# Attention with a layer norm in front: scores in two groups of three units over three PSUM banks instead of three groups of two, with other steps moved in each engine's order

## The reference

```python
h = jnp.maximum(_layernorm(x, axis=-1), 0.0)
q = _heads(h @ Wq + bq)
k = _heads(h @ Wk + bk)
v = _heads(h @ Wv + bv)
scores = jnp.einsum('bhqd,bhkd->bhqk', q, k) / np.sqrt(HEAD_SIZE)
bias = jnp.where(graph_mask, 0.0, NEG)[:, None]
probs = jax.nn.softmax(scores + bias, axis=-1)
ctx = jnp.einsum('bhqk,bhkd->bhqd', probs, v)
out = x + ctx @ Wf + bf
```

## Time and profile before

| | us |
|---|---|
| three executions: median (lowest to highest) | 593.15 (592.7 to 593.23) |
| the profiled execution | 594.17 |
| its span, first to last instruction | 592.4 |
| PE busy in it | 575.3 |
| ACT, POOL, DVE busy | 516.3, 491.4, 473.5 |

### The profile page before, as it was taken

The page is one execution under the profiler, slowest core; times in us unless marked ns, Lnnn a source line. Parts: engine busy times, 40 slices in busy tenths (PEclk is TensorE's granted clock), DMA queues, the critical chain, the costliest instruction groups (busy, mean ns, idle before and its releaser), DMA issues.

```text
span 592.4 us, 17738 instructions
## 1 busy us (share of the span) xinstructions
PE 575.3 (97%) x6640; PEld 429.6 (73%) x6640; DVE 473.5 (80%) x1484; ACT 516.3 (87%) x1161; POOL 491.4 (83%) x533
## 2 busy tenths in 40 slices
PE   7997999999999999999999999999999999999986
PEld 7676777777777777777777777776777777777754
DVE  5988888888878878888887888888787778878664
ACT  2788999899999999999999999998999999999972
POOL 2779998888899888889988888988888898888870
PEclk9999999999999999999999999999999999999999
DMA  8048889879788989879897977789897787978662
GB/s 273 8 77 148 134 169 177 170 159 168 165 148 157 185 157 178 167 141 168 160 184 157 181 163 150 159 158 177 165 178 166 157 151 161 179 132 153 125 133 73
DMA packets 275640, 92.01 MB, mean 155 GB/s; under 512 B 257633, under 2 KB 275554, under 8 KB 275554
## 3 DMA queue, kind: packets, MB, share of 16 engines
q1 hardware_dynamic: 274352, 90.87, 79.8%
q10 hardware_dynamic: 1202, 0.01, 0.1%
HBM read 17.05 MB, written 12.58 MB: 50 GB/s over the span
## 4 chain that ended last, share of the span: by engine, by line
PE 82%; DVE 6%; ACT 5%; DMA 3%; issue 2%; POOL 1%; ACTq 0%; SPq 0%; DVEq 0%; POOLq 0%
PE ring L1043 18%; PE ring L1045 18%; PE ring L1044 18%; PE scores L1106 11%; PE ctx L1129 5%; PE ring L1141 3%; PE ctx L1131 3%; PE ctx L1130 3%; DMA p_cols<-p_rows 2%; DVE logits L750 2%; ACT probs L550 2%; DVE h_rows L767 1%; DMA bf_row<-in_L_gnn_bf_dram 1%; ACT qk L575 1%; PE ring L1171 1%
## 5 line engine op out<-in xcount | busy, mean ns | idle before, releaser
L428 POOL TENSOR_TENSOR p_rows<-probs,p_rows 128x512 f16<-128x512 f32 x190 | 220.6, 1161 | 32.2 <-ACT p_rows L555 31.8
L750 DVE CUSTOM_DVE_ANT_0 logits<-scores,mask,logit_unscale 128x256 f32<-128x256 f32 x384 | 169.0, 478 | 61.6 <-PE scores L1106 61.4
L550 ACT ACTIVATE probs<-logits,raised 128x256 f32<-128x256 f32 x372 | 168.9, 501 | 6.0
L1043 PE MATMUL ring<-h_cols,w_hi 128*128 128x256 f16 x576 | 157.2, 273 | 0.0
L1045 PE MATMUL ring<-h_cols,w_lo 128*128 128x256 f16 x576 | 157.0, 273 | 0.0
L1044 PE MATMUL ring<-h_cols,w_hi 128*128 128x256 f16 x576 | 156.9, 272 | 0.0
L414 POOL TENSOR_TENSOR split<-qk,split 128x512 f16<-128x512 f32 x96 | 111.5, 1161 | 36.4 <-DVE split L774 36.4
L555 ACT ACTIVATE p_rows<-probs 128x512 f16<-128x512 f32 x190 | 119.7, 630 | 6.0
L575 ACT ACTIVATE qk<-ring,qk_bias_s,qkv_ratio 128x256 f32<-128x256 f32 x192 | 96.5, 552 | 3.7 <-PE ring L1045 3.7
L1129 PEld LDWEIGHTS ctx<-v_hi,p_cols 128*128 128x128 f16 x756 | 68.9, 97 | 33.2 <-issue 27.7
L1129 PE MATMUL ctx<-v_hi,p_cols 128*128 128x65 f16 x756 | 88.2, 195 | 4.1 <-DMA p_cols<-p_rows 2.0
(11 more groups left out here) (116 smaller groups left out, 1158.6 us busy)
## 6 DMA issues: line engine op xcount, KB each, us to landing
x_in<-in_x_dram SPq DMA_DIRECT2D x32, 384.0 KB, 3.9
out_dram<-result SPq DMA_DIRECT2D x62, 192.0 KB, 2.2
p_cols<-p_rows SPq DMA_TRANSPOSE x190, 3.2
adj_in<-in_adj_dram SPq DMA_DIRECT2D x32, 64.0 KB, 2.9
w_raw<-in_L_gnn_Wq_dram SPq DMA_DIRECT2D x1, 576.0 KB, 5.6
w_raw<-in_L_gnn_Wv_dram SPq DMA_DIRECT2D x1, 576.0 KB, 8.0
w_raw<-in_L_gnn_Wf_dram SPq DMA_DIRECT2D x1, 576.0 KB, 9.0
h_cols<-h_rows SPq DMA_TRANSPOSE x29, 4.7
```

Source lines behind the costliest of these rows:

```text
L428: pool.tensor_tensor(p_rows[u][:, 1], probs[u % 3][:], p_rows[u][:, 0], ALU.subtract).then_inc(p_lo_ready, 1)
L550: act.activation(probs[u % 3][:, a], logits[u % 3][:, a], ACT.Exp, bias=raised[u % 3][:, a:a + 1], scale=-1.0).then_inc(probs_ready, 1)
L750: dve.tensor_tensor_reduce(out=logits[u % 3][:, a], in0=score_bank[a][:, u % 2 * S:(u % 2 + 1) * S], in1=mask[b.parity][:, t], scale=logit ...
L1043: pe.matmul(out_ap, a_hi, m_hi, start=first, stop=False)
```

## The change

- The scores banks are three, `scores0` to `scores2`; the third is the bank that was `peaks`. A group of scores is the three units of one query tile, 18 matmuls, at `attend(0)` and `attend(3)`. Unit 0 writes banks 1 and 2, unit 1 banks 0 and 2, unit 2 banks 0 and 1. Bank 1 is thus written by the lower half of the array for unit 0 and by the upper half for unit 2, so unit 2's first matmul of head 1 waits for a new semaphore, `shared_bank_done`, which the last matmul of unit 0 and head 0 raises.
- Batch 0 makes its scores in four groups, of the units 0 and 1, 2, 3, and 4 and 5.
- DVE: `mask_and_max` of unit 2 stands ahead of `v_lo_part`, `h_lo_rows` behind unit 3 and `divide` instead of behind unit 2, `layer_stats` ahead of `qk_hi_part`. ACT: `h_hi_rows` stands behind unit 2 instead of ahead of `context_hi` and unit 2. POOL: `add_bias` (the next input) stands behind `probs_lo` of unit 4, and `split_lo` of pair 2 ahead of it. SP: the transpose of unit 2 stands ahead of that of `h`.
- The last batches use other banks, and on DVE the division of batch 30 stands ahead of `mask_and_max` of unit 1 of batch 31.

```diff
-    GROUPS = UNITS // 2
+    GROUPS = UNITS // C
-        score_bank = [bank("scores0"), bank("scores1")]
-        peak_bank = bank("peaks")
+        score_bank = [bank(f"scores{n}") for n in range(3)]
+        peak_bank = score_bank[2]
...
+        def score_of(u, a):
+            n, column = ((1, 0), (2, 0), (0, 0), (2, S), (0, S), (1, S))[u % C * 2 + a]
+            return score_bank[n][:, column:column + S]
...
+        def scored(b, u):
+            if b.k == 0:
+                return (1, 1, 2, 3, 4, 4)[u]
+            return 4 + (b.k - 1) * GROUPS + u // C + 1
@@ SP, cycle @@
+                if here:
+                    transpose_probs(b, 2)
                 if (b + 2).exists():
                     transpose_h(b + 2)
-                if here:
-                    transpose_probs(b, 2)
@@ POOL, cycle @@
                 if here:
                     probs_lo(b, 3)
                 if front:
+                    split_lo(b + 1, 2)
+
+                if here:
+                    probs_lo(b, 4)
+                if front:
                     add_bias(b + 1)
-
-                if here:
-                    probs_lo(b, 4)
-                if front:
-                    split_lo(b + 1, 2)
@@ ACT, cycle @@
                 if front:
                     qk_full(b + 1, 0)
+                if before:
+                    context_hi(b + -1, 0)
+                if here:
+                    exps(b, 2)
+                    probs_hi(b, 2)
                 if (b + 2).exists():
                     h_hi_rows(b + 2)
-                if before:
-                    context_hi(b + -1, 0)
-                if here:
-                    exps(b, 2)
-                    probs_hi(b, 2)
@@ DVE, cycle @@
                 if here:
+                    mask_and_max(b, 2)
                     v_lo_part(b, 0)
                     v_lo_part(b, 1)
                 if b.k == 1:
                     weights_lo(3, 8)
-                if here:
-                    mask_and_max(b, 2)
+                if (b + 3).exists():
+                    layer_stats(b + 3, (0,))
                 if front:
                     qk_hi_part(b + 1, 0)
                 if before:
                     context_lo(b + -1, 0)
-                if (b + 2).exists():
-                    h_lo_rows(b + 2)
                 if here:
                     mask_and_max(b, 3)
                 if before:
                     divide(b + -1, 1)
+                if (b + 2).exists():
+                    h_lo_rows(b + 2)
                 if front:
                     qk_hi_part(b + 1, 1)
-                if (b + 3).exists():
-                    layer_stats(b + 3, (0,))
-
                 if here:
                     mask_and_max(b, 4)
-                if front:
-                    qk_hi_part(b + 1, 2)
                 if (b + 3).exists():
                     layer_stats(b + 3, (1,))
                     layer_moments(b + 3)
+                if front:
+                    qk_hi_part(b + 1, 2)
@@ DVE, last batch @@
             mask_and_max(LAST, 0)
+            divide(PREV, 0)
             mask_and_max(LAST, 1)
-            divide(PREV, 0)
+            mask_and_max(LAST, 2)
             finish(PREV + -1, 1)
             v_lo_part(LAST, 0)
             v_lo_part(LAST, 1)
-            mask_and_max(LAST, 2)
@@ PE @@
+            def scores(b, units):
+
+                for u in units:
...
+                wait(pe, logits_ready, b.count(2 * UNITS, 2 * units[0]))
+                for u in units:
                     t, tile = u // C, split[b.parity][u % C]
                     for n, (q, k) in enumerate(((1, 2), (1, 3), (0, 2))):
                         for a in range(2):
+                            if u % C == 2 and n == 0 and a == 1:
+
+                                wait(pe, shared_bank_done, b.count(GROUPS, u // C + 1))
                             own = slice(D * a, D * a + D)
+                            mm = pe.matmul(score_of(u, a), tile[own, q, t * P:(t + 1) * P], tile[own, k],
                                            start=(n == 0), stop=(n == 2))
+                            if u % C == 0 and n == 2 and a == 0:
+                                mm.then_inc(shared_bank_done, 1)
                 mm.then_inc(scores_ready, 1)
@@ PE, batch 0 @@
-            scores(Batch(0), 0)
+            pe.wait_ge(peaks_joined, 2)
+            scores(Batch(0), (0, 1))
...
-            scores(Batch(0), 1)
+            scores(Batch(0), (2,))
...
+            scores(Batch(0), (3,))
             project_qk(Batch(1), 1)
-            scores(Batch(0), 2)
+            scores(Batch(0), (4, 5))
@@ PE, cycle @@
-                    if here and u % 2 == 0:
-                        scores(b, u // 2)
+                    if here and u % C == 0:
+                        scores(b, range(u, u + C))
@@ PE, last batch @@
-            scores(LAST, 0)
+            scores(LAST, range(0, C))
             apply_probs(PREV, 2)
             project_out(PREV + -1, 1)
             apply_probs(PREV, 3)
-            scores(LAST, 1)
             transpose_context(PREV, 0)
             apply_probs(PREV, 4)
-            scores(LAST, 2)
+            scores(LAST, range(C, UNITS))
             apply_probs(PREV, 5)
```

More of the change, by code:

```diff
@@ L201, in gnn_attention @@
         scores_ready = sem("scores_ready")
+        shared_bank_done = sem("shared_bank_done")
         logits_ready = sem("logits_ready")
@@ L707, in context_hi_last @@
                 act.activation(ct_hi[1][:, chunks].rearrange("p c q -> p (c q)"),
-                               R_CT[1][:, chunks.start * P:chunks.stop * P], ACT.Copy).then_inc(ct_hi_ready, 1)
+                               ct_of(LAST, 1)[:, chunks.start * P:chunks.stop * P], ACT.Copy).then_inc(ct_hi_ready, 1)
             exps_last(0)
@@ L742, in mask_and_max @@
                 t, j = u // C, u % C
-                wait(dve, scores_ready, b.count(GROUPS, u // 2 + 1))
+                wait(dve, scores_ready, scored(b, u))
                 if u == 0:
@@ L1092, in project_v @@
                     mm.then_inc(v_ready, 1)
-            def scores(b, g):
-                for u in (2 * g, 2 * g + 1):
+            def scores(b, units):
+                for u in units:
                     if u < C:
@@ L1099, in scores @@
                         wait(pe, qk_lo_ready, b.count(C, u + 1))
-                wait(pe, logits_ready, b.count(2 * UNITS, 4 * g))
-                for u in (2 * g, 2 * g + 1):
+                wait(pe, logits_ready, b.count(2 * UNITS, 2 * units[0]))
+                for u in units:
                     t, tile = u // C, split[b.parity][u % C]
@@ L1135, in transpose_context @@
                 wait(pe, context_ready, b.count(2, t + 1))
-                if t == 0 and (b + -1).exists():
-                    wait(pe, result_ready, (b + -1).count(2, 2 if b.k < B - 1 else 1))
+                if t == 0 and b.k == B - 1:
+                    pe.wait_ge(logits_ready, b.count(2 * UNITS, 2 * UNITS))
+                elif t == 0 and (b + -1).exists():
+                    wait(pe, result_ready, (b + -1).count(2, 2))
                 if t == 1 and (b + 2).exists():
@@ L1140, in transpose_context @@
                 for c in range(C):
[L1141 removed]
+                    mm = pe.transpose(ct_of(b, t)[:, c * P:(c + 1) * P],
                                       context[t][:, 2 * c:2 * c + 2].rearrange("p h d -> p (h d)"), ident[:])
@@ L1146, in project_out @@
                 wait(pe, ct_lo_ready, b.count(2, t + 1))
-                if t == 1 and b.k < B - 2:
+                if t == 1:
                     wait(pe, result_ready, b.count(2, 1))
+                elif b.k == B - 1:
+                    pe.wait_ge(result_ready, PREV.count(2, 2))
                 for c in range(C):
@@ L1263, in turn_probs @@
                 else:
-                    pe.wait_ge(logits_ready, LAST.count(2 * UNITS, 2 * UNITS))
+                    pe.wait_ge(logits_ready, LAST.count(2 * UNITS, 2 * UNITS - 2))
                 for a in range(2):
@@ L1282, in project_out_last @@
                 pe.wait_ge(ct_lo_ready, LAST.count(2, nth))
-                pe.wait_ge(result_ready, PREV.count(2, 2))
                 for c in range(chunks.start, chunks.stop):
```

33 lines of the change are left out of this document (16 added, 17 removed).

## The result

The changed kernel takes 597.06 us (median of 7 runs, 595.5 to 599.22); the kernel before, on the same chip, 592.83 (7 runs, 592.43 to 593.23). The ratio is 1.0067, with a 95% interval of 1.0055 to 1.008: the change makes the kernel 0.7% slower, where 586.7 was forecast. The profiled execution took 597.02 us, its span is 595.2. (The medians are 4.2 us apart and the two profiled spans 2.8, because the profiled execution of the kernel before, 594.17, was slower than its median.

What follows compares the result with a forecast made beforehand. PE's own instruction stream was taken as the bound. Group gain −7.5, late transposes +2.3, bank wait +0.3, long cycles −0.8, head −0.4, tail −0.3 sum to −6.4: 593.15 − 6.4 = 586.7 us, range 582 to 591.

Steps and rivals of the forecast that it cites:

- What is late next: Unit 1's DMA transpose, issued at 8.8, wanted at 13.75: lateness 0.08 us a cycle on average, 2.3 us in all.
- if the landing times grow with the denser issue: DMA transposes: the condition under which the prediction said it would be wrong above all; no size given.
- The rival that held: PE waits for unit 1's or unit 0's transpose in most cycles, 0.2 us each: 590.2 us, chance 0.12.
- The gain of a group: PE's scores, one group less in a cycle: 0.26 us a cycle gained, 7.5 us in all (5.8 to 7.5).
- The timetable: Starts worked out for the new cycle: second group at 7.96, next cycle at 17.0 to 17.05 us.
- `shared_bank_done`: PE's wait inside a score group: 0.3 us expected; the rival, a stall of 0.2 a group, 598.9 us, chance 0.07.
- The increment on a matmul in mid-stream: Semaphore increment added in each score group: costed at nothing; by the skill page 1.6 us, sum 587.8.
- DVE and ACT: Pace with three units at a time: 1.3 us of cover on DVE, 1 us left on ACT a cycle.
- the 1.2 us of cover worked out for the split: POOL's split of pair 2 ends at about 15.8, 1.2 us before the next first group wants it.
- Head: Start of the run: one more group in batch 0, one wait for `least` gone, net −0.4 us.
- Tail: Last batches: shorter waits mostly come back in one piece, same clock fall expected, net −0.3 us.

Runs made afterwards that it cites:

- only_groups: The changed kernel's banks, groups, head and tail, with the cycle orders of DVE, ACT, POOL and SP as in the kernel before: 636.2 us, ratio 1.0734.
- late_apply: The changed kernel with PE's block for unit 1 moved behind the context transpositions and two thirds of v's first half: 584.88 us, ratio 0.9856.
- res_gap: The changed kernel with POOL's residual moved into an idle stretch ahead of the split of pair 1: 610.08 us, ratio 1.0292.
- before_x_early: The kernel before with the load of x behind unit 4's transpose from the second cycle on: 593.03 us, ratio 0.9995.
- before_want_early: The kernel before with unit 1's probabilities applied ahead of the output projection, 1.46 us earlier: 596.98 us, ratio 1.0081.
- only_orders: The kernel before, its two banks and three groups kept, with the changed kernel's cycle orders of DVE, ACT, POOL and SP: 615.73 us, ratio 1.0394.
- x_behind: The changed kernel with SP's load of x moved from ahead of unit 1's transpose to behind unit 2's: 592.13 us, ratio 0.9996.
- x_early: The changed kernel with the load of x behind unit 4's transpose and ahead of unit 5's from the second cycle: 586.16 us, ratio 0.9875.

## Why the prediction was wrong

**The step that failed** is "What is late next". It forecast the right transfer, the right issue (8.8; the median is 8.7) and the right want (13.75), and bounded the lateness of a cycle by 0 and 1.1. Then it took 0.08 us a cycle, 2.3 in all, "since the median is far on the good side". Measured: 0.39 a cycle, 11.2 in all, and 1.7 in the worst cycle, beyond the upper bound. That difference, 8.9 us, is most of the 10.4 us between forecast and result. It has three parts, which can be worked out as sums over 29 cycles of max(0, issue + landing − 13.75):

- The wrong sample. The median of 3.2 was that of all 190 transposes. Unit 1's stands right behind the load of x in 26 of the 29 cycles. Before the change too, its own median was 4.25, with six of the 29 above 5 us and the longest 6.0. With those landings and an issue at 8.8 the sum is 3.6 us. So the right 29 landings would have given a third of the loss, and their median alone nothing, since 8.8 + 4.25 is less than 13.75: where the median lies under the limit, the tail decides.
- Longer landings, the largest part. In the trace of the changed kernel unit 1's median is 4.62, with ten above 5 us and the longest 6.6. With these the sum is 9.0. The prediction named this as what it would be wrong by, "if the landing times grow with the denser issue", and gave it no price of its own. Why they grew stays open. There is one trace of each kernel, and in the others that keep the load ahead of unit 1 between 6 (only_groups) and 12 (late_apply) of the 29 are above 5 us, so part of the growth may be chance.
- Later issues. They are not always at 8.8, but as late as 9.74. With the measured ones the sum is 11.1.

**The rival that held** was the wait for unit 1's transpose, at 0.12 and 590.2. It has the mechanism, though it said "in most cycles" and 12 of 29 were long. Its size, 0.2 a cycle, rested on "a PE that waits gives POOL the same time back, so that about half of a lateness remains". None of it was given back in the same cycle: 1.57 us late, 1.58 longer. What a wait gives is slack for the next cycle: unit 1's issue stands at 8.25 behind a long cycle and at 8.99 behind another (medians), and only two of the twelve long cycles follow a long one.

**The gain of a group** was right: 17.05 for a cycle that waits for nothing, as forecast (17.0 to 17.05), against 17.26 to 17.31 before; a group of 18 takes 1.18 from the end of the last slot ahead of it (317.00 + 0.11) to the next block at 318.29, forecast 1.2. The timetable was right to 0.1: second group at 8.05 (7.96).

**`shared_bank_done`** (rival at 0.07, 598.9): no stall. The group's records end 1.16 after its start, and 8 pairs of steps of 0.11 and one matmul of 0.28 are 1.16. The result is close to that rival's 598.9, and the cause is another: read a time alone and the wrong theory would seem confirmed. The increment on a matmul in mid-stream costs nothing that shows, as the waitless cycles are as forecast. (The sum that the prediction gives with 1.6 us for these increments, 587.8, should read 588.3, 586.7 + 1.6; the 1.6 did not appear.)

**DVE and ACT** kept pace with three units at a time: no wait for `least` is left. POOL kept pace as well, by the 1.2 us of cover worked out for the split; it goes when a two-input instruction of DVE runs beside POOL's, as in res_gap.

**Head**: forecast −0.4, measured 64.36 against 63.64, +0.7. The first cycle waits for unit 1's transpose as well (issued at 55.29, landed in 5.7). Without that wait, in late_apply, the group starts at 62.88, 0.8 earlier than before. Not all of such a difference need come from the change: in before_x_early, with the head of the kernel before, it starts at 64.1, 0.5 later.

**Tail**: forecast −0.3, measured −0.8 (from 569.94 to the end 25.26, before 26.05). That it comes near is luck. The waits of 1.0 for `least` and 0.7 for `context` went, and a wait of 1.6 for `result` came in their place. What is left is the clock: I had expected the same fall as before, and it did not come. The windows that answer to the earlier trace rows:

```profile
570.00:575.00 5.00, 3.40 (x52) 2.33 (x52) 3.83 (x16) 2.87 (x7) 3.45 (x6) 1.00 0.81 140
575.00:580.00 5.00, 3.98 (x57) 2.94 (x58) 3.89 (x16) 4.43 (x10) 3.32 (x7) 1.00 0.83 129
```

But that fall does not belong to the kernel before. before_x_early has the same last batches, and in its trace they run from 566.95 to 591.95, 25.0 us, with the clock at 1.00:

```profile
575.00:580.00 5.00, 4.14 (x56) 3.33 (x56) 3.70 (x13) 4.06 (x10) 2.35 (x4) 1.00 0.88 181
```

The tails of before_want_early and only_orders, also those of the kernel before, take 25.0 too. So at the same clock the changed tail is 0.25 longer, and the −0.8 is a fall of the clock that one execution of the kernel before had.

The sum closes: head +0.7, cycles +2.9, tail −0.8, together +2.8, the 595.2 − 592.4 of the spans. With the tail at the same clock it is 3.9, near the 4.2 between the medians.

## What to carry to other kernels

Before an order is made denser, take for each transfer that will have less slack the landings of that very transfer in the trace, with its tail and what its queue issues just ahead, not those of its kind: here the limit lay above the median and inside the tail. Leave room beyond them, as they would have given 3.6 of the 11.2 us. Then look for slack at either end, as both worked here: move the big load off the queue's critical place (−10.9 us), or let the consumer do other work first (−12.2 us, one block moved on one engine). And when work is moved into an idle stretch of POOL, look at what DVE does in that stretch: two-input instructions of both engines side by side can cost more than the idle time gives.

## What the runs showed of the hardware

- A DMA transpose of the same size landed in 3.05 us (x_behind and x_early, medians) when the load was not issued just ahead of it, mostly in 4.1 to 4.8 behind the load of x, and in up to 6.6. What makes the last 2 us was read and not tried. Of unit 1's 29 landings in the changed kernel, 17 have a packet of an instruction queue 1.7 to 4.2 us after their issue, and all ten above 5 us are among these. In late_apply it is so for only seven of the twelve above 5 us. The DMA view of the stretch from 194.6 to 200.9 us (busy tenths in 40 slices; packets, MB, share):

```profile
DMA  9997792244769999999992019999999500000009
...
q1 hardware_dynamic: 2278, 1.05, 105.9%
q8 instruction: 1, 0.02, 1.1%
q14 instruction: 1, 0.01, 0.6%
```

  Whether these packets hold the transfer up, or only come in the same stretches, stays open.
- A short DVE instruction with two inputs in SBUF took as long as POOL's instruction beside it had left: 0.88 us for 8 columns, whose shortest took 0.15.
- A wait inside a run of matmuls on the engine's own semaphore, met just ahead of it, cost nothing that a record shows: 1.16 us for the records of a group of 18, as the sum of its steps.
- Stretches that look alike go either way with the clock. With PE busy 3.40 of 5.00 us (after) and 3.41 of 5.00 (before_x_early) the granted clock of TensorE stayed at 1.00, the level of 2.4 GHz; in the kernel before, PE was busy 3.38 of 5.10 and the clock fell to 0.56 in the next 3.9 us, although before_x_early runs the same instructions there. So a fall in one trace is no property of a kernel, and a tail should be compared at the same clock.
